# One block for set-up and attention, written-out closing steps, blanks two at a time, first rows in halves, three last sums on TensorE

## What is computed

```python
h = layernorm(x) * (1 + ca) + sa
q, k, v = heads(h @ wq.T), heads(h @ wk.T), heads(h @ wv.T)      # 16 heads of 64
phi_q, phi_k = exp(q @ omega.T - |q|^2 / 2) / 8, the same for k   # 64 features
out = phi_q @ cumsum(phi_k x v) / (phi_q . cumsum(phi_k) + 1e-6)  # causal, linear
x = x + bound(ga) * (out @ wo.T + bo)
h = layernorm(x) * (1 + cb) + sb
scores = softmax(h @ wg)             # 8 experts, the best 2 of each token
slot of a token in its expert = its place in line, dropped from place 1024 on
y = (gelu(rows @ w1 + b1) @ w2 + b2) * weight
x = x + bound(gb) * (y of first choice + y of second choice)
```

## Time and profile before

| | |
|---|---|
| three runs | 801.48, 803.26, 806.25 us (median 803.26) |
| profiled execution, its own time | 799.26 us |
| its span, first to last instruction | 797.5 us |
| busy in the span: PE, DVE, ACT, POOL | 90%, 69%, 49%, 44% |
| mean granted clock of PE | 0.964 |

### The profile page before, as it was taken

How to read it: one execution, slowest core, us unless ns; L and a number is a source line. 1 busy time by engine, 2 the same in 40 slices (tenths; PEclk the granted TensorE clock), 3 DMA queues, 4 the chain that set the end, 5 groups by cost and what they waited for, 6 DMA issues and landing times. The chain is left out here.

```text
span 797.5 us, 28182 instructions
## 1 busy us (share of the span) xinstructions
PE 716.2 (90%) x11303; PEld 598.2 (75%) x11303; DVE 546.9 (69%) x1745; ACT 391.9 (49%) x740; POOL 348.6 (44%) x640
## 2 busy tenths in 40 slices
PE   6789999999999999999999999999997459999930
PEld 6568888887787787888877788787886448999930
DVE  5467777777777777777777777777775425565518
ACT  3555555555555555555555555555552115444310
POOL 2362444444444444444444444444444322556550
PEclk9999999999999999999999999999999569999985
DMA  9890000000000000000000000000000044545128
GB/s 260 330 370 3 10 9 10 10 10 9 10 13 13 9 10 9 10 8 10 9 10 9 13 13 10 8 10 9 10 9 10 8 114 137 166 141 162 56 72 284
DMA packets 44696, 47.31 MB, mean 59 GB/s; under 512 B 4092, under 2 KB 36000, under 8 KB 44568
## 3 DMA queue, kind: packets, MB, share of 16 engines
q1 hardware_dynamic: 35184, 32.69, 12.9%
q0 software_dynamic: 4096, 8.42, 3.3%
q10 hardware_dynamic: 5288, 4.40, 1.7%
HBM read 22.21 MB, written 23.36 MB: 57 GB/s over the span
## 5 line engine op out<-in xcount | busy, mean ns | idle before, releaser
L1100 POOL DMA_INDIRECT y_rows<-y_sb,row_id x64 | 63.1, 986 | 65.3 <-DVE y_sb L1215 47.6
L917 POOL TENSOR_TENSOR both<-prob 128x1 f32<-128x1 f32 x32 | 6.1, 190 | 195.1 <-ACT prob L687 195.1
L935 POOL DMA_INDIRECT dispatched<-h_cur,slot x64 | 66.9, 1046 | 21.2 <-issue 20.3
L1163 ACT ACTIVATE hidden<-bank,b_col 128x512 f32<-128x512 f32 x64 | 44.0, 687 | 57.4 <-PE bank L1144 54.8
L603 PE MATMUL bank<-woT,attT 128*128 128x128 f32 x512 | 67.3, 286 | 1.0 <-ACT attT L682 1.0
L697 ACT ACTIVATE h_full<-bank,sa_col,ca_col 128x192 f32<-128x192 f32 x32 | 16.4, 511 | 101.5 <-PE bank L620 101.5
L726 DVE TENSOR_REDUCE norm_q<-square_q 128x16 f32<-128x1024 f32 x32 | 39.0, 1220 | 39.0 <-ACT square_q L648 39.0
L603 PEld LDWEIGHTS bank<-woT,attT 128*128 128x128 f32 x512 | 61.2, 196 | 3.2 <-DVE taken L801 0.8
L1119 PE MATMUL bank<-w_sb,hidden 128*128 128x128 f32 x512 | 59.7, 275 | 0.9 <-issue 0.9
L1119 PEld LDWEIGHTS bank<-w_sb,hidden 128*128 128x128 f32 x512 | 58.4, 192 | 1.3 <-issue 1.3
L640 ACT ACTIVATE phiT_k<-bank 128x512 f32<-128x512 f32 x64 | 38.2, 597 | 42.4 <-PE bank L460 42.4
(11 more groups left out here) (225 smaller groups left out, 2069.5 us busy)
## 6 DMA issues: line engine op xcount, KB each, us to landing
dispatched<-blank SPq DMA_DIRECT2D x16, 524.0 KB, 6.3
region<-dispatched SPq DMA_DIRECT2D x31, 262.0 KB, 3.5
y_rows<-blank SPq DMA_DIRECT2D x8, 512.0 KB, 7.6
w_nat<-in_L_ffn_w_dram SPq DMA_DIRECT2D x8, 256.0 KB, 4.3
y_got<-y_rows ACTq DMA_DIRECT2D x8, 256.0 KB, 7.5
y_got<-y_rows SPq DMA_DIRECT2D x8, 256.0 KB, 6.8
out_dram<-x_sb SPq DMA_DIRECT2D x8, 256.0 KB, 3.5
w_sb<-in_L_ffn_w_dram ACTq DMA_DIRECT2D x6, 256.0 KB, 3.3
```

Source lines behind the costliest of these rows:

```text
L935: pool.indirect_dma_start(out=dispatched[:, :], in_=h2_cur[par][:], in_offset=None, out_offset=bass.IndirectOffsetOnAxis(ap=slot[par][:, k ...
L1100: pool.indirect_dma_start(out=y_rows[:, :], out_offset=bass.IndirectOffsetOnAxis(ap=row_id[par][:, t:t + 1].bitcast(U32), axis=0), in_=y_s ...
L1163: act.activation(hidden[par][:, k, :], psum[2 + k][:], ACT.Gelu, bias=b1_col[:, bass.ds(e * KH + k, 1)]).then_inc(sem(f"hid{k}_out"), 1)
```

## The change

It does seven things.

1. Set-up and attention become one block. Each engine's function `opening` holds the old set-up and steps -2 and -1, interleaved by hand; the weights now go through banks 2 to 5 so that banks 0 and 1 are free for projections. The steps then run from c = 0. Each projection of chunk 0 waits only for its own weights (`SPLIT`). PE begins with 16 transposes of the identity.
2. SP loads the first three chunks of x before wk and wv. The 24 blank writes follow the loads with no meeting of the engines between, and write n waits until write n - 2 has landed (`two_at_most`).
3. The bounding of the gates moves from POOL (ten instructions) to DVE (three for each gate, and the copy of b1 ahead of them), in steps 0 and 1.
4. The last two steps of PE are written out (`closing_steps`), with transposes of the identity that nothing reads between the real work (`keep_busy`: 6, 6, 6, 24, 6, 12 and 48 of them). In step 32, DVE finds chunk 30's slots ahead of the last heads' sum, and POOL does chunk 30's weights and scatter before it waits for chunk 31's x.
5. The experts' first group loads in halves: two tiles of each region with a semaphore of their own (`first_in`), which DVE merges and PE transposes before the other two.
6. `WARM` goes from 32 to 40, and PE does 120 transposes of the identity (`CLOSING`) after the last product.
7. In passes 3, 5 and 7 (`BY_PE`) PE adds the two sums in a bank, as products with the identity, and DVE multiplies from the bank.

The core of the difference:

```diff
+                        def opening():
+
+                            pe.wait_ge(sem("ident_ready"), 2)
+                            for i in range(16):
+                                pe.transpose(psum[7][:, 0:P], ident[:], ident[:])
+                            pe.wait_ge(sem("wq_loaded"), 16)
+                            weights(0)
+                            weights(1)
+                            small()
+                            first_T(0)
+                            pe.wait_ge(sem("small_used"), 3)
+                            weights(2)
+                            weights(3)
+                            pe.wait_ge(sem("h_split"), 1)
+                            project("q0", -1, 0)
+                            project("q1", -1, 0)
+                            pe.wait_ge(sem("kv_loaded"), 32)
+                            weights(4)
+                            weights(5)
+                            weights(6)
+                            project("k0", -1, 0)
+                            project("k1", -1, 0)
+                            weights(7)
+                            project("pq1", -1, 0)
+                            project("pq0", -1, 0)
+                            weights(8)
+                            weights(9)
+                            modulation(0)
+                            first_T(1)
+                            project("pk0", -1, 0)
+                            project("pk1", -1, 0)
+                            modulation(1)
+                            project("v0", -1, 0)
+                            project("v1", -1, 0)
+                            modulation(2)
+                            modulation(3)
+                            closing_weights()
...
+                        def keep_busy(n):
+
+                            for i in range(n):
+                                pe.transpose(psum[BANK["tk0"]][:, 0:P], ident[:], ident[:])
...
+                        def closing_steps():
+
+                            c, par = NCH, NCH % 2
+                            attend_state(1, c - 1, 1 - par, CPB - 1)
+                            keep_busy(6)
+                            attend(1, c - 1, 1 - par, CPB - 1)
+                            routing_T(c, par)
+                            keep_busy(6)
+                            routing_logits(c)
+                            attended_T(0, c)
+                            attended_T(1, c)
+                            routing_rank(c)
+                            keep_busy(6)
+                            pe.wait_ge(sem("rank_out"), c - 1)
+                            add_heads(c)
+                            c, par = NCH + 1, 1 - par
+                            keep_busy(24)
+                            routing_T(c, par)
+                            keep_busy(6)
+                            routing_logits(c)
+                            keep_busy(12)
+                            routing_rank(c)
+                            keep_busy(48)
+
                         def step(c, b, j):
+                            if isinstance(c, int) and c >= NCH:
+                                if c == NCH:
...
+                            if isinstance(c, int) and c == 0:
+                                pe.wait_ge(sem("mod_used"), 4)
...
+                                pe.wait_ge(sem("woT_ready"), 2)
...
+                        def bound_gate(m):
+
+                            t = (ga_b, gb_b)[m]
+                            g = t[:, 0:B * D]
+                            dve.wait_ge(sem("mod_used"), 4)
+                            if m == 0:
+                                dve.wait_ge(sem("small_filled"), 3)
+                                dve.tensor_copy(b1_col[:], psum[6][:, 0:E * KH])
+                            dve.tensor_scalar(sgn[:], g, 0.0, -0.5, ALU.is_ge, ALU.add).then_inc(sem("d_chain"), 1)
+                            dve.wait_ge(sem("d_chain"), 3 * m + 3)
+                            dve.scalar_tensor_tensor(out=mag[:], in0=g, scalar=4.0, in1=sgn[:], op0=ALU.mult, op1=ALU.mult).then_inc(sem("d_chain"), 1)
+                            dve.wait_ge(sem("d_chain"), 3 * m + 4)
+                            dve.scalar_tensor_tensor(out=g, in0=mag[:], scalar=0.5, in1=sgn[:], op0=ALU.max, op1=ALU.mult).then_inc(sem("d_chain"), 1)
...
+                            condition(0)
+                            condition(1)
+                            weight_lo(0)
+                            condition(2)
+                            dve.wait_ge(sem("x_begun"), 16)
+                            first_moments(dve, 0)
+                            weight_lo(1)
+                            first_norm(dve, 0, 0)
+                            condition(3)
+                            first_moments(dve, 1)
+                            weight_lo(2)
+                            first_norm(dve, 1, 1)
+                            weight_lo(3)
+                            sum_squares("q", -1)
+                            weight_lo(4)
+                            weight_lo(5)
+                            weight_lo(6)
+                            sum_squares("k", -1)
+                            weight_lo(7)
+                            exponent("q", 1, -1)
+                            exponent("q", 0, -1)
+                            weight_lo(8)
+                            weight_lo(9)
+                            first_moments(dve, 2)
+                            exponent("k", 0, -1)
+                            exponent("k", 1, -1)
...
+                            if isinstance(c, int) and c < 2:
+                                bound_gate(c)
...
+                            if isinstance(c, int) and c == NCH:
+                                find_slots()
...
                             if isinstance(c, int) and c == NCH:
+                                pool.wait_ge(sem(f"sent{nxt}"), 32 * ((c - 1) >> 1))
+                                pool.tensor_copy(h2_cur[nxt][:, D:D + 1], token[:, c - 1:c])
+                                find_weights()
+                                scatter()
                                 pool.wait_ge(sem("x2_ready"), c)
                                 rstd(pool, "ln2", var2, rs2, c)
                                 pool.tensor_copy(x_sb[:, (c - 1) * D:c * D], x2_now[:])
-                                find_weights()
-                                pool.wait_ge(sem(f"sent{nxt}"), 32 * ((c - 1) >> 1))
-                                pool.tensor_copy(h2_cur[nxt][:, D:D + 1], token[:, c - 1:c])
-                                scatter()
                                 return
...
+                            pool.wait_ge(sem("p_chain"), 6)
+                            low(0)
+                            rstd(pool, "ln1", var1, rs1, 2)
+                            low(1)
+                            rstd(pool, "ln1", var1, rs1, 3)
...
+                        sp.wait_ge(sem("ident_ready"), 1)
+                        for i in range(2):
+                            sp.dma_start(om_blk[i * M:(i + 1) * M, i * DH:(i + 1) * DH], omega).then_inc(sem("s_om"), 16)
+                        x_piece(0)
+                        for k, w in (("k", wk), ("v", wv)):
+                            sp.dma_start(w_nat[k][:], w.rearrange("(j p) d -> p j d", p=P)).then_inc(sem("kv_loaded"), 16)
+                        sp.dma_start(wo_nat[:], wo).then_inc(sem("wo_loaded"), 16)
+                        sp.dma_start(b1_nat[:], b1.rearrange("e (k p) -> (e k) p", p=P)).then_inc(sem("wo_loaded"), 16)
+                        for i in range(1, len(X_PIECES)):
+                            x_piece(i)
...
+                        def two_at_most(n):
+
+                            if n >= 2:
+                                sp.wait_ge(sem(f"blanked{n % 2}"), n // 2 * 16)
...
-                WARM = 32
+                WARM = 40
+                FIRST = GS // 2
+                CLOSING = 120
...
+                def first_rows(eng, k, part):
+
+                    tiles = slice(part * FIRST, (part + 1) * FIRST)
+                    eng.dma_start(region[k][0][:, tiles, :], slot_rows[:, k * NSL + part * FIRST:k * NSL + (part + 1) * FIRST, :])\
+                       .then_inc(sem("region_in0" if part else "first_in"), 16)
...
+                            if isinstance(g, int) and g == 0:
+                                pe.wait_ge(sem("first_merged"), 1)
+                                for t in range(FIRST):
+                                    pe.transpose(psum[par][:, t * P:(t + 1) * P], rows[par][:, t, 0:D], ident[:])
...
+                        for i in range(CLOSING):
+                            pe.transpose(psum[5][:, 0:P], ident[:], ident[:])
+                        for i in BY_PE:
+                            bank = psum[2 + BY_PE.index(i)]
+                            pe.wait_ge(sem(f"y_loaded{i}"), 32)
+                            for k in range(2):
```

(13 more changed lines are left out.)

587 lines of the change are left out of this document (306 added, 281 removed).

## The result

The changed kernel takes **793.27 us** (median of 4 executions, 791.03 to 796.49) beside 804.05 (4 executions, 801.48 to 806.25) of the kernel before on the same chip: ratio 0.9879, 95% interval 0.9847 to 0.9911. It is faster by 10.8 us, 1.2%; 792.8 was predicted. The profiled execution took 791.03 us, with a span of 789.3 us, 8.2 less than the 797.5 of before.

The account below looks back on a forecast made before the run. PE was taken to bound steps 2 to 30 (busy 504.0 of 512 us), leaving savings elsewhere: 4.5 + 0.1 + 2.6 + 1.2 + 2.1 = 10.5 us, off the median 803.26 gives 792.8 us; 8-in-10 range 787 to 799.

Parts of the forecast that it names:

- Opening: Until step 0's first q projection: it starts at 32.3 instead of 36.83, 4.5 us gained; bounds 1.7 and 6.0.
- the layout of the first 13 us: Chunk 0 normalised at 10.8, omega products at full speed until 13.2, first projection then instead of at 25.64.
- a sign of being wrong: Start of step 0: a start after 35 would show the forecast wrong; 31 to 34 was expected.
- Steps 0 and 1: Gates moved to DVE cost time, the `h_lo` and issue waits go: net 0.1 us gained; bounds 1.0 lost, 1.8 gained.
- Steps 2 to 30: The middle, PE busy 504.0 of 512 us: no instruction changed, so 18.4 us each as before, 0 gained.
- Closing: Last attention steps: chunk 31's weights no longer wait for POOL, 2.6 us gained; bounds 1.5 and 3.4.
- Experts' start: Block's start to w1's first product: 7.1 us instead of 8.3, 1.2 gained; 0.6 lost at half clock, upper bound 1.8.
- End: Last sums on DVE: three passes lose their sum to PE, 2.1 us gained; bounds 0.4 and 2.2.
- just in time: Last sums: pass 3's data land near 782.5, PE's products take 1.8 us, DVE's turn is 784.4.
- Rival 1: Clock stays low in closing, experts' start and end: 5.9 us gained, 797.4 us; chance 0.19.
- Rival 2: Opening stays where it was, step 0 at 35.1 or later: 1.7 us or less gained there, about 795.6; chance 0.11.
- Rival 4: Slower: blank writes throttle POOL, deciding from 4.3 us a blank; 807.8 us at 4.6; chance 0.04.

Follow-up runs that it names:

- a_warm_open: The changed kernel with 34 more idle transposes on PE between the small products and chunk 0's transpose in the opening; 792.2 us.
- a_blanks_deep: The changed kernel with SP no longer holding a blank write back until the one two before it has landed; 792.88 us.
- a_no_keep: The changed kernel without the closing's idle transposes and with 32 instead of 40 ahead of the experts; 798.18 us.

## Why the prediction was right, and where only its total was

The total, 10.5 us, met 10.8. Its terms did less well: in the two profiles those of the change come to 5.7 us, and the total owes a good part to luck.

- **Opening, 4.5: measured 2.1.** The step that failed is the layout of the first 13 us: "11.3, then 13.2 at full speed", and DVE taking moments at once. x's first piece landed 1.65 us late for DVE, PE stood 4.13, and the products ran at 3.63. The fall of the clock was named as the lower bound and should have been the value: the layout itself had PE waiting from 8.3 to 10.8. a_warm_open prices it at 1.5; chunk 0 itself reached PE 1.1 later than laid out (11.92 for 10.8). Behind chunk 0's projection the layout was good: 18.8 us to step 0, 19.1 predicted, k's low half waited for 1.92, predicted 1.7. Step 0's start, 34.74 here and 34.1 to 36.5 over nine profiles with this opening, lies beyond the 31 to 34 of the forecast, and in four of the nine past the 35 that was to be a sign of being wrong.
- **Steps 0 and 1, 0.1: measured 0.9.** The four parts as written add up to 0.2. The wait for `h_lo` went and DVE's gates cost 0.8 in step 0, as said; in step 1 they cost 0.2 at most, not 0.6. The step that failed is the credit for the issue wait of 0.93 to the gentler blanks: a_blanks_deep has none either, and five profiles with the blanks two by two have one. It comes and goes.
- **Steps 2 to 30, 0: measured 2.5.** No instruction differs; most steps take 18.3 in both profiles, and the profile of before has single steps of 18.9, 18.9 and 19.5, the last with a wait for issue of 0.92. This is the luck of the two executions, as far as can be told, and not the change.
- **Closing, 2.6: measured 3.2.** Root behind scatter, POOL idle for the exponents, 3.2 us from exponents to scatter: all as said; a_no_keep shows that this order is worth 2.6 by itself. Chunk 31's h came 1.4 earlier and not 0.3, since the clock stayed up from step 31's products of scores and v on; in the profiles where it fell there, h came 0.2 earlier, though w_o's products took 1.95 in them too.
- **Experts' start, 1.2: measured 1.0**, at full clock, as said; without the transposes it is 1.5 longer (a_no_keep).
- **End, 2.1: measured -1.4.** The failed step is "just in time". A pair at half clock, 3.6, and its lateness, 1.4, were only in the lower bound (3.9 and 1.88 measured). And that bound of 0.4 gained was itself too high: its own numbers make pass 3 late by 1.7 (782.5 + 3.6 - 784.4), and it counted pass 3's data as landed 8.2 after the issue (782.5 - 774.25), where they take 9.8. From the issue on it is 9.8 + 3.9 + 8.2 = 21.9 against 20.48.
- **Rivals.** Rival 1 is half true: but for some 3 us behind the wait at 626.93 the clock stayed up in closing and start, and it fell at both ends, opening and last sums. Rival 2's mark, a start at 35.1 or later, was missed by 0.4 in the changed kernel's profile and met in three of the nine. Rival 4 can be ruled out: 1.8 us a blank.
- **Total.** The profiled execution saved 8.2 where the sum said 10.5. The medians differ by 10.8 because the profile of before came from an execution 4.8 under its median, and that of after from one 2.2 under. Carrying the sum over to the median was right by 2.6 us of such luck. And since the terms of the change make 5.7 of the 8.2, the other 5 of the 10.8 are not located: of the kernel before only this short execution left a profile.

## What to carry to other kernels

Where PE waits for a landing or another engine ahead of work on the path, price that work at both speeds and look which one the traces bear out for a wait of that length: here it ran at half speed behind every wait of the opening and of the last sums (2.8 to 6.7 and 3.6 to 5.0 us), behind eight of twelve of 2.5 in the closing, and behind two of ten of 1.6 in step 0. Count idle work put in front of it against the landing, from the issue on. A sum given to a second engine pays only for data that have landed well before the first engine's turn: late passes, not early ones. Before crediting a change with a wait that it removes, look whether the wait comes back at the same instruction in other executions.
